# A small GpSimd memset behind every indirect gather of a two-layer graph network kernel

## The reference, cut to what matters

```python
# layer 0
Q, K, V = x @ WQ, x @ WK, x @ WV;  Eh = edge_attr @ WE
score = exp(clip((K[src] * Q[dst] / sqrt(dh) * Eh).sum(-1), -5, 5))      # 8 heads
h = x + segment_sum(V[src] * score, dst) / (segment_sum(score, dst) + 1e-6)
# layer 1
xl = x @ W;  e = leaky_relu(a_src[src] + a_dst[dst], 0.2)
e = exp(e - segment_max(e, dst)[dst])
out = segment_sum(e / segment_sum(e, dst)[dst] * xl[src], dst) + bias     # then two dense layers
```

## Time and profile before

| what | value |
|---|---|
| median of 3 executions | 4707.78 us (4704.26 to 4708.37) |
| the profiled execution: span from first to last instruction | 4693.0 us |
| own time of the profiled execution | not listed apart from the three above; the median lies 14.8 us over its span |
| gathers of layer 0, first to last start | 81.05 to 2286.13 us |
| gathers of layer 1, first to last start | 2443.83 to 4538.89 us |
| GpSimd busy | 3369.7 us (72%) |
| TensorE busy | 3812.3 us (81%) |
| VectorE busy | 3158.1 us (67%) |
| ScalarE busy | 1078.1 us (23%) |

### The profile page before, as it was taken

The page is one execution under the profiler, slowest core; times in us unless marked ns, Lnnn a source line. Parts: engine busy times, 40 slices in busy tenths (PEclk is TensorE's granted clock), DMA queues, the critical chain, the costliest instruction groups (busy, mean ns, idle before and its releaser), DMA issues. The chain is left out here.

```text
span 4693.0 us, 76906 instructions
## 1 busy us (share of the span) xinstructions
PE 3812.3 (81%) x19332; PEld 3161.6 (67%) x19333; DVE 3158.1 (67%) x8279; ACT 1078.1 (23%) x4010; POOL 3369.7 (72%) x3437
## 2 busy tenths in 40 slices
PE   6889899989989988888898977777777777777778
PEld 5777777777778877767567755655555556555555
DVE  1877677677777776777646866666666666666657
ACT  3100010000000000000034433333333333333324
POOL 3677777777777777777557777777777777777752
PEclk9887787787776787888687555555555555555559
DMA  7666665666666666666424322222222222222224
GB/s 279 182 182 184 176 189 176 179 183 181 183 181 182 182 183 174 185 179 183 148 86 97 61 61 61 61 61 61 61 61 61 61 61 60 60 61 61 61 58 154
DMA packets 376029, 593.47 MB, mean 126 GB/s; under 512 B 151298, under 2 KB 204520, under 8 KB 374488
## 3 DMA queue, kind: packets, MB, share of 16 engines
q0 software_dynamic: 132880, 330.18, 27.4%
q1 hardware_dynamic: 241544, 255.24, 18.2%
q10 hardware_dynamic: 1552, 7.43, 0.4%
HBM read 551.16 MB, written 40.54 MB: 126 GB/s over the span
## 5 line engine op out<-in xcount | busy, mean ns | idle before, releaser
L393 POOL DMA_INDIRECT kv_g<-kv_table,idx x1661 | 1678.2, 1010 | 568.0 <-issue 498.7
L1065 POOL DMA_INDIRECT xg<-xl_table,idx x1661 | 1583.0, 953 | 519.3 <-issue 498.6
L1130 PEld LDWEIGHTS ps_sum<-pw,xg 128*128 128x128 f32 x3328 | 740.9, 328 | 165.9 <-DVE pws L1271 165.5
L1130 PE MATMUL ps_sum<-pw,xg 128*128 128x64 f32 x3328 | 819.1, 428 | 4.7 <-DVE pws L1271 2.2
L452 PE MATMUL ps_sum<-kv_g,hot 128*64 128x136 f32 x3328 | 606.6, 339 | 246.8 <-issue 245.8
L1117 PE MATMUL ps_tops<-ident,top 128*64 128x128 f32 x832 | 285.9, 447 | 518.7 <-DVE top L1243 518.4
L452 PEld LDWEIGHTS ps_sum<-kv_g,hot 128*64 128x64 f32 x3328 | 480.9, 167 | 314.9 <-issue 310.2
L438 PE MATMUL ps_pair<-w,eat 128*128 128x128 f32 x3328 | 616.3, 342 | 5.1 <-issue 5.1
L438 PEld LDWEIGHTS ps_pair<-w,eat 128*128 128x128 f32 x3328 | 524.2, 240 | 109.3 <-issue 71.7
L442 PE MATMUL ps_pair<-qw,hott 64*128 64x128 f32 x3328 | 583.9, 326 | 2.9 <-DMA qw<-q_table 2.9
L1229 DVE SCALAR_TENSOR_TENSOR ps_lg<-raw 128x256 f32<-128x256 f32 x416 | 185.3, 445 | 573.4 <-ACT raw L1178 566.7
(11 more groups left out here) (160 smaller groups left out, 4684.9 us busy)
## 6 DMA issues: line engine op xcount, KB each, us to landing
eat<-in_edges SPq DMA_DIRECT2D x416, 256.0 KB
local<-local_table SPq DMA_DIRECT2D x416, 128.0 KB, 3.8
kv_g<-kv_table,idx POOLq DMA_INDIRECT x1661
xg<-xl_table,idx POOLq DMA_INDIRECT x1661
qw<-q_table SPq DMA_DIRECT2D x416, 32.0 KB
adw<-ad_row SPq DMA_DIRECT2D x416, 32.0 KB, 5.1
kv_table<-kv_out SPq DMA_DIRECT2D x25, 512.0 KB, 2.6
xl_table<-xl SPq DMA_DIRECT2D x25, 264.0 KB, 2.8
```

Of the source, the lines that this page charges most:

```text
L393: nc.gpsimd.indirect_dma_start(out=kv[:, u, k, 0:2 * D], out_offset=None, in_=m["kv_table"], in_offset=bass.IndirectOffsetOnAxis(ap=idx[:, ...
L1065: nc.gpsimd.indirect_dma_start(out=xg[:, u, k], out_offset=None, in_=m["xl_table"], in_offset=bass.IndirectOffsetOnAxis(ap=idx[:, u // B, ...
L1130: nc.tensor.matmul(ps_sum[:, b, 0:W], xg[:, u, k, 0:D], pw[:, b, k], start=(k == 0), stop=(k == K - 1))
```

## The change

In both edge parts a tile of 32 values in each of the 128 partitions is added (`rest0`, `rest1`), with a semaphore each, which starts at 1. Behind each gather GpSimd now waits until the memset behind the gather before it is complete, raises the counter `passed`, and clears the tile. Nothing reads the tile. The far-window routines have no memset.

```diff
@@ edges0 @@
+        rest0, rested0 = sb("rest0", [P, 32]), sem("rested0")
...
+            lead(pool, [rested0], 1)
+
             def gather(c, v, last=False):
...
                         in_offset=bass.IndirectOffsetOnAxis(ap=idx[:, i, u * K + k:u * K + k + 1],
                                                             axis=0)).then_inc(kv_in[u], 16)
+                    pool.wait_ge(rested0, c * K + k + 1)
+                    alone(pool, m["passed"])
+                    nc.gpsimd.memset(rest0[:], 0.0).then_inc(rested0, 1)
@@ edges1 @@
+        rest1, rested1 = sb("rest1", [P, 32]), sem("rested1")
...
+            lead(pool, [rested1], 1)
+
             def gather(c, u, last=False):
...
                         in_offset=bass.IndirectOffsetOnAxis(ap=idx[:, u // B, u % B * K + k:u % B * K + k + 1],
                                                             axis=0)).then_inc(xl_in[u], 16)
+                    pool.wait_ge(rested1, c * K + k + 1)
+                    alone(pool, m["passed"])
+                    nc.gpsimd.memset(rest1[:], 0.0).then_inc(rested1, 1)
```

## The result

The changed kernel takes 4760.74 us, the median of three executions (4754.11 to 4765.77), against 4707.78 us: a ratio of 1.0117, 95% interval 1.0099 to 1.0136. It is slower, as forecast, but by 53 us and not by 242: the time lies 9 us under the lower end of the range. The profiled span grew from 4693.0 to 4752.1 us, by 59.1 us.

The account below looks back on a forecast made before the run. The prediction took GpSimd's issue of gathers as the bound: 3,226 gathers at 0.075 us add 242 us to the profiled 4693.0, giving 4935, plus 14.8 to the median: 4950 us, range 4773 to 5385 us.

Parts of the forecast that it names:

- The bound: In both layers GpSimd's issue of gathers sets the pace, although TensorE's busy share (81%) is higher than GpSimd's (72%).
- The increment and the wait at nothing: Behind each gather, the added semaphore increment and wait are sequencer work, covered by the previous gather's 0.94 us: cost nothing.
- The memset's term: Between gathers, each memset holds GpSimd for 0.075 us, in series: 242 us over 3,226 gathers.
- Rival 2: The memset hides in the 0.30 us gap before each gather; spacing stays 1.25 us, time 4708 us; chance 0.09.
- The number of gathers: Only gathers after the buffer rings first fill pay for their memset: 1,629 in layer 0 and 1,597 in layer 1.
- The second term: Layer 0 gathers held up by VectorE, 106 us in all: left at no change, ends between -106 and +81 us.
- the first: Changing instruction kinds is dear: each gather behind a memset pays 0.11 us more, 5305 us, or gaps, 6063 us; chance 0.13.
- the fourth: TensorE stays at the low clock in layer 0, some 580 us more: 5290 us; chance 0.01.
- The test of the reasoning: From filled ring to last gather, each layer's stretch grows by the number of gathers times the growth of the spacing.
- the signs that I had named: Layer 1 spacing 1.32 to 1.33 us; consumers' row waits about 0.3 us longer per chunk; TensorE's layer 0 clock lower.

Follow-up runs that it names:

- e7: The kernel before the change with two more counter increments behind each gather, no memset and no wait: 4711.92 us, beside 4707.09 us.
- e8: The kernel before the change with six more counter increments behind each gather, no memset and no wait: 4714.25 us, beside 4707.09 us.
- e16: The kernel before with the change's tiles and semaphores, two increments and a wait for a constant behind each gather, no memset: 4702.31 us, beside 4706.88 us.
- e13: The kernel before the change with the change's tiles and semaphores declared but unused: 4705.53 us, ratio 1.0000.
- e1: The change with each memset waiting for the eighth memset before in layer 0, the second before in layer 1: ratio 1.0120 to the kernel before.
- e4: The change with the memset 128 wide in layer 0 and 4 wide in layer 1, in place of 32: 5789.53 us, where the kernel before took 5,692 to 5,742.

## Why the prediction was right and wrong

**The bound** was right. GpSimd's issue of gathers sets the pace in both layers, and the time grew with it: 23.3 and 39.3 us between the filled rings and the last gathers, of 59.1 us. The consumers wait more and GpSimd waits less, as said.

**The increment and the wait at nothing** was right for the work that they are: two increments more per gather leave the spacing alone (e7), six add 0.002 to 0.003 us (e8), and a met wait for a constant adds nothing (e16). It was wrong for what the wait does to the order, and this is the larger miss, 50 of the 59 us. "They are covered by the 0.94 us in which the gather before is still at work" took the cover of one gather for enough. The sequencer was 13 gathers ahead before the change and is one ahead after it, and its pauses, 18 and 28 of them, need two.

**The memset's term** failed as well, and it is the step on which the sum rests: "I take 0.075 us, from the row nearest in kind". The row was of two ordinary instructions in a row; a gather is not one. The runs show a sum with a floor. A gather starts 0.17 us after the end of the memset or 1.25 us after the gather before, whichever is later, and so 0.13 us of memset are free. Its cost is 0.0065 us on average, 21 us in all instead of 242. Rival 2 had the mechanism and got 0.09. The argument against it, that a gap which never varies looks like the beginning of the gather itself, holds for 0.17 of the 0.30 us and not for the rest. I had 0 and 0.42 us as bounds and no row between them that was taken beside a gather; with such a gap in the trace, "fits in the gap" deserved about the chance of the forecast. My guess of the memset's duration, 0.12 us, was near the 0.14 measured.

**The number of gathers** that count, 1,629 and 1,597, was right: the rings fill as before and GpSimd idles 20.45 and 6.31 us there.

**The second term**, the gathers held up by VectorE in layer 0, was left at no change, and their mean is 1.009 us after 1.010. That hides two movements: the plain gathers (those under 0.97 us) take 0.952 us after 0.946, and what the others lose beyond the plain duration falls from 107 to 94 us. And I looked at layer 0 alone. In layer 1 the gather's mean rose from 0.953 to 0.964 us, 17.7 us over all; some 10 us of this are the plain gathers (0.951 us after 0.945), and the rest, from gathers that lose 21 us beyond the plain duration after 14, is no effect of the change: e13, with GpSimd's instructions of before, loses 21 us as well.

**Of the rivals**, the first and the fourth are out: no gather behind a memset pays 0.11 us, and in layer 0 TensorE was granted 0.78 after 0.77, not less. In the stretch from 500 to 2000 us, columns as in the earlier trace rows, the change above and the kernel before below:

```profile
500.00:2000.00 1500.00, 1313.40 (x7898) 1129.56 (x7897) 1084.61 (x2258) 139.41 (x564) 1310.01 (x2255) 0.78 0.62 179
```

```profile
500.00:2000.00 1500.00, 1340.83 (x7996) 1153.03 (x7994) 1095.03 (x2283) 141.23 (x570) 1152.39 (x1142) 0.77 0.63 181
```

**The test of the reasoning** that I had set, that the stretches grow by the number of gathers times the growth of the spacing, fails: 12 and 10 us by that rule, 23.3 and 39.3 measured. The term that was missing altogether is the long spacings, 50 us. Had they not come, the change would have cost some 10 us, about what a measurement can tell from nothing. So "slower" came true for a reason that the prediction does not have, and that was luck. Of the signs that I had named, the spacing came out at 1.256 us and not at 1.32 to 1.33, the consumers' waits for rows grew by 53/416 = 0.13 and 40/416 = 0.10 us per chunk and not by 0.3, and TensorE's granted clock did not fall.

## What to carry to other kernels

An idle gap of constant length before an instruction is not all its own beginning. Part of it can be free; what is put there costs only what goes beyond the free part, and a run with two widths finds where that is. A wait that is always met, and a sequencer instruction that costs nothing, can still cost time: they decide how far the sequencer may run ahead, and that lead hides its pauses. When a regular pace is disturbed, look at the spacings one by one and at the distance between the odd ones: 46 gaps among 3,322 made more than two thirds of this change's cost, and no mean or group shows them. And before an experiment rules a theory out, look whether the run has the state that the theory speaks of: e1 allowed a lead of eight gathers and had one of one or two.

## What was not expected of the hardware

- The floor of 0.17 us from the end of a memset to the start of a gather, in four widths from 32 to 256 columns, beside the 0.30 us from gather to gather. Behind the memset of 4 columns it is 0.19 us (e4, layer 1).
- The pause of GpSimd's sequencer, every 88 gathers of 256 values a row and every 56 of 132, which shows as a gap of 1.72 or 0.97 us where the sequencer is one gather ahead and not at all where it is two ahead.
- How far that sequencer runs ahead of the gathers where no wait holds it: 12 to 13 gathers, some 15 us.
- A memset can be held up by VectorE. Here is one in layer 0, and VectorE beside it:

```profile
1303.79 0.95 POOL L396 DMA_INDIRECT kv_g<-kv_table,idx  x1 [0.17 <-POOL rest L402]
1304.73 0.31 POOL L402 MEMSET rest<- 128x32 f32 x1
1305.04 1.37 POOL L396 DMA_INDIRECT kv_g<-kv_table,idx  x1
```

```profile
1304.41 0.57 DVE L561 TENSOR_SCALAR hott<-local,line 64x512 f32<-64x512 f32 x1
1304.91 0.67 DVE L582 TENSOR_TENSOR kv_g<-kv_g 128x512 f32<-128x512 f32 x1
```

Between 500 and 2000 us 93 of the 101 memsets that began inside L561 took over 0.18 us, and none of the 155 that began inside L582, which has two inputs in SBUF. The gather behind starts without any gap, so this costs nothing: 1303.79 to 1305.04 is 1.25 us again. The Trainium skill (SBUF — State Buffer, Who interferes with whom) says both: that a VectorE instruction with two SBUF inputs does not hold up a GpSimd instruction that only writes, and that a tensor_scalar in one of the two-port modes does. This trace agrees with the first by its 0 of 155; the second names the kind of instruction that held the memsets up here; whether L561 ran in such a mode no view shows.
- The same program and chip took 4,707 us on one occasion and 5,742 us on another, where TensorE's counter `summed` rose some 5 us late and the engines stood still together for it; what sets this off no run here shows.
